# Row casts of the DMA-turned attention steps on GpSimd, and earlier query products in the indexer

## The reference

```python
q_lat = rmsnorm(hidden_states @ q_a_w, q_a_norm_w)
q = (q_lat @ q_b_w).reshape(b, s, H, QKD).transpose(0, 2, 1, 3)      # 32 heads, 128 + 64 (rope)
kv = (rmsnorm(kv_lat, kv_a_norm_w) @ kv_b_w)...
scores = (q_nope @ k_nope^T + rope(q_pe) @ rope(k_pe)^T) * QKD ** (-0.5)
idx_scores = einsum(iw, relu(iq @ ik^T)) * IDX_D ** (-0.5)           # 16 indexer heads of 128
_, topk_idx = top_k(where(causal, idx_scores, -inf), 128)
attn = softmax(where(topk_mask & causal, scores, -inf))
x = x + (attn @ v) @ o_w + experts(xn)                                # top 2 of 8, rank 16
```

## Time and profile before

| | |
|---|---|
| median of 3 runs | 975.35 us |
| the profiled execution | 986.95 us, of which the span is 985.2 us |
| PE busy | 842.8 us (86%), granted clock 0.96 over the span |
| DVE busy | 703.7 us (71%) |
| ACT busy | 654.1 us (66%) |
| POOL busy | 462.3 us (47%) |
| DMA transposes (L443) | 64 |

### The profile page before, as it was taken

The page is one execution under the profiler, slowest core; times in us unless marked ns, Lnnn a source line. Parts: engine busy times, 40 slices in busy tenths (PEclk is TensorE's granted clock), DMA queues, the critical chain, the costliest instruction groups (busy, mean ns, idle before and its releaser), DMA issues.

```text
span 985.2 us, 20194 instructions
## 1 busy us (share of the span) xinstructions
PE 842.8 (86%) x7496; PEld 502.2 (51%) x7496; DVE 703.7 (71%) x1589; ACT 654.1 (66%) x1388; POOL 462.3 (47%) x343
## 2 busy tenths in 40 slices
PE   4969989876666989888988999999999998829998
PEld 2436444443334555555554665665666665614443
DVE  5366678899999999999997777777777767620100
ACT  3657789865664878788877877887877887820000
POOL 2193388853443555455554556556556555310000
PEclk9999999978896999999999999999999999959999
DMA  7012111112332444444441665565775555670211
GB/s 231 22 44 86 55 54 44 59 38 61 99 90 65 124 125 124 117 124 118 135 123 45 135 129 118 115 120 106 130 133 118 113 118 111 119 227 1 64 43 43
DMA packets 168609, 96.66 MB, mean 98 GB/s; under 512 B 116544, under 2 KB 142528, under 8 KB 168512
## 3 DMA queue, kind: packets, MB, share of 16 engines
q1 hardware_dynamic: 168512, 95.37, 39.9%
HBM read 36.62 MB, written 6.29 MB: 44 GB/s over the span
## 4 chain that ended last, share of the span: by engine, by line
PE 44%; DVE 26%; issue 11%; ACT 10%; POOL 7%; DMA 2%; SPq 0%; POOLq 0%; DVEq 0%; ACTq 0%
PE psS L690 9%; PE psS L762 9%; DVE arena L1236 6%; DVE arena L1041 6%; ACT arena L793 6%; PE psT L746 5%; DVE m L1173 3%; POOL bias L1415 3%; DVE bias L1180 2%; PE psS L577 2%; PE psT L564 2%; PE psT L544 2%; ACT arena L978 2%; POOL arena L1349 2%; PE psO L717 2%
## 5 line engine op out<-in xcount | busy, mean ns | idle before, releaser
L690 PE MATMUL psS<-keyT,arena 128*128 128x512 f16 (+3 forms) x1152 | 231.4, 329 | 18.8 <-DVE small L1236 14.8
L978 ACT ACTIVATE arena<-arena,small 128x512 f32<-128x512 f32 (+7 forms) x256 | 198.2, 774 | 66.3 <-DVE small L1241 37.5
L1041 DVE SCALAR_TENSOR_TENSOR arena<-psT,arena 128x512 f16<-128x512 f32 (+3 forms) x278 | 146.8, 548 | 107.1 <-ACT arena L793 105.9
L793 ACT ACTIVATE arena<-psT 128x512 f16<-128x512 f32 (+4 forms) x360 | 171.8, 505 | 49.6 <-PE psT L613 25.5
L1236 DVE CUSTOM_DVE_ANT_0 arena<-psS,bias 128x512 f32<-128x512 f32 (+7 forms) x256 | 191.9, 750 | 0.1
L577 PE MATMUL psS<-ikT,big 128*128 128x512 f16 (+3 forms) x528 | 112.0, 359 | 38.1 <-DVE bias L1126 34.6
L746 PE MATMUL psT<-ident,arena 128*128 128x128 f32 x736 | 115.9, 278 | 22.1 <-DVE arena L1041 18.1
L690 PEld LDWEIGHTS psS<-keyT,arena 128*128 128x128 f16 x1152 | 91.4, 98 | 75.1 <-DVE small L1236 18.0
L1415 POOL TENSOR_TENSOR bias<-arena,bias 128x768 f32<-128x768 f32 (+2 forms) x48 | 91.3, 1916 | 58.4 <-ACT arena L859 58.1
L746 PEld LDWEIGHTS psT<-ident,arena 128*128 128x128 f32 x736 | 84.6, 141 | 55.2 <-ACT arena L978 30.9
L577 PEld LDWEIGHTS psS<-ikT,big 128*128 128x128 f16 x528 | 51.2, 104 | 91.2 <-DVE bias L1126 42.3
(11 more groups left out here) (162 smaller groups left out, 1406.5 us busy)
## 6 DMA issues: line engine op xcount, KB each, us to landing
arena<-arena SPq DMA_DIRECT2D x192, 128.0 KB, 2.4
arena<-in_wiq SPq DMA_DIRECT2D x32, 256.0 KB, 2.7
arena<-in_ow SPq DMA_DIRECT2D x16, 512.0 KB, 3.5
arena<-in_qbT SPq DMA_DIRECT2D x16, 256.0 KB, 2.5
wvo_parts<-arena SPq DMA_DIRECT2D x16, 256.0 KB, 2.0
arena<-in_qpe SPq DMA_DIRECT2D x16, 128.0 KB, 2.9
arena<-in_x SPq DMA_DIRECT2D x8, 256.0 KB, 3.3
out<-arena SPq DMA_DIRECT2D x8, 256.0 KB, 2.1
```

The source lines that it names most:

```text
L690: last = mm(bank[:, k:k + w], Q[:, u % 2, h, a, q:q + P], keyT[:, b, h, k:k + w], start=(a, b) == (0, 0), stop=(a, b) == (1, 0))
L793: return nc.scalar.activation(dst, src, ACT.Copy, scale=scale)
L978: nc.scalar.activation(pr[:, g % 4, 0:kw], pr[:, g % 4, 0:kw], ACT.Exp, bias=shift[:, g % 4:g % 4 + 1], scale=-1.0, accum_out=rsum[:, unit ...
L1041: return v.scalar_tensor_tensor(out=dst, in0=src, scalar=scale, in1=hi, op0=ALU.mult, op1=ALU.subtract)
```

## The change

There are two parts. The first takes the fp16 row cast of the 64 DMA-turned steps out of ScalarE's program and puts it into GpSimd's, straight ahead of the subtraction of the same row; the wait for the row buffer to be free goes with it. The second moves the query jobs of the first two units to other heads of the indexer's last third, and with them the swaps and placings in SyncE's order and GpSimd's and ScalarE's steps for them.

```diff
-        FIRST = {4: ("R", 0), 6: ("L", 0), 9: ("R", 1), 12: ("L", 1)}
+        FIRST = {2: ("R", 0), 4: ("L", 0), 7: ("R", 1), 10: ("L", 1)}
...
                 load_qw(p, p % 2, False)
-                if p == 7:
+                if p == 5:
                     swap(0)
+                if p == 8:
+                    place(0, latent, qa_lo, q_lat, 1)
                 if p == 10:
-                    place(0, latent, qa_lo, q_lat, 1)
+                    swap(1)
+                if p == 11:
                     place(0, turned, q_rot, q_tur, 0)
-                if p == 13:
-                    swap(1)
...
-                if n in (8, 13):
-                    rope_hi((8, 13).index(n))
+                if n in (7, 12):
+                    rope_hi((7, 12).index(n))
...
-            def rows_hi_(g):
-
-                kw, d = P * (tile_of(g) + 1), TURN_AT[g]
-                if d >= 3:
-                    act.wait_ge(landed[(d - 3) % 4], landed_by(d - 3))
-                act.wait_ge(exp_done, g + 1)
-                copy(rows_of_turn(d)[:, 0:kw], pr[:, g % 4, 0:kw], 1.0).then_inc(row_hi, 1)
...
                     exp_step(g + AHEAD - 1)
-                    if turns(g + AHEAD - 1):
-                        rows_hi_(g + AHEAD - 1)
...
             def rows_lo_(x):
                 kw, d = P * (tile_of(x) + 1), TURN_AT[x]
+                if d >= 3:
+                    pool.wait_ge(landed[(d - 3) % 4], landed_by(d - 3))
+                pool.wait_ge(exp_done, x + 1)
+                g.tensor_copy(rows_of_turn(d)[:, 0:kw], pr[:, x % 4, 0:kw]).then_inc(row_hi, 1)
                 pool.wait_ge(row_hi, d + 1)
...
-                if n in (6, 11):
-                    rope_cos((6, 11).index(n))
-                    rope_sin((6, 11).index(n))
+                if n in (4, 9):
+                    rope_cos((4, 9).index(n))
+                    rope_sin((4, 9).index(n))
+                if n in (6, 12):
+                    q_low((6, 12).index(n))
                 if n in (8, 13):
-                    q_low((8, 13).index(n))
                     rope_low((8, 13).index(n))
```

More of the change, by code:

```diff
@@ L1005, in _ @@
                 exp_step(g)
-                if turns(g):
-                    rows_hi_(g)
             for g in range(STEPS):
```

## The result

The changed kernel is 0.67% faster: the ratio of its times to those of before is 0.9933, with a 95% interval of 0.9911 to 0.9955 (20 runs of each; medians 972.86 and 979.94 us, means 973.60 and 980.22, which give that ratio). That is 6.6 us, where the sum came to 14 us. The first three runs of before (975.35) lie at the fast end of its times: the twenty go from 974.81 to 988.58 us, those of the changed kernel from 970.33 to 979.38.

A forecast was written before the change was run, and what follows sets the result against it. VectorE was taken to bound the indexer's last third, TensorE attention's second half. Terms of -8 and -6 us made -14 against the profiled 986.95 us (-1.42%); that share of the timed 975.35 gave 961, range 949 to 975.

The forecast's parts named there:

- Part 2: Indexer's last third: query jobs moved to heads 2, 4, 7, 10 free three heads, 2.0 us each, 6 us gained.
- Part 1: Attention's second half: row casts moved to GpSimd save 12.2 us, 4 given back, so 8 us gained.
- the late queries: Attention's second half: the next unit's queries land after TensorE is ready, giving back 4 us, between 0 and 12.
- the chain to the R job: Attention's second half: ScalarE's 1024-column cast delays a copy, VectorE's rest and TensorE's query job, 0.81 us a unit, 12.2 us.
- Rival (a): Attention: GpSimd's cast costs as much as its subtraction, 2.13 us, so queries land late; 980 us, slower; chance 0.12.
- The margin: Attention's second half: queries land at 653.3 by the median placing, TensorE reads them at 654.04, so 0.7 us to spare.
- the other 48 casts: Attention: casts of a unit's other three turned steps are off TensorE's critical waits; their removal gains nothing.
- Head 2 is freed: Indexer's last third: the query job delays GpSimd's join 3 past VectorE's rests of head 2, gaining 2.0 us.
- Join 4 comes 7.6 us behind the accumulation of head 2: Indexer's last third: GpSimd's join of head 4 starts after VectorE's rests of head 3, gaining another 2.0 us.
- At head 4 the job of the latents has the same effect: Indexer's last third: the latent query job at head 4 frees VectorE's rests from a join, gaining 2.0 us.
- as even: Indexer's last third, from head 5 on: no net gain or loss assumed, since TensorE's granted clock changes between levels.
- Rival (b): Indexer's last third: new joins meet VectorE's rests at other heads, costing 4 us; 971 us; chance 0.15.

The follow-up runs named there:

- the queries early: Changed kernel, second half of attention: next unit's query placings ahead of step 1's transposing DMA, rope cast and rope_low also moved ahead; ratio to before 0.98.
- Without collisions: Kernel before, with GpSimd's joins in the indexer's last third adding only 64 of 1024 columns; ratio to before 0.987.

## Why the prediction was wrong, step by step

Two terms of the sum failed. Part 2 was to give 6 us and gave nothing: its chain of joins and rests was wrong from the second link on. Part 1 was to give 8 us and gave 6: the late queries were taken too small.

- **TensorE is the bound of the second half, and the 1024-column cast is on the chain to the R job: right.** The wait is gone in every unit, and the cast alone gives the effect. Its worth was 0.97 us a unit, where the idle time gave 0.81: 14.6 us in place of 12.2.
- **The cast on GpSimd: right, and cheap.** 1.04 us, forecast 1.23 (bounds 1.0 and 2.13); the four widths give 0.84 ns a column and 0.18 us fixed, where the forecast had 1.05 and 0.15. Rival (a) needed 1.8 us and falls.
- **The queries land late: right in kind, the term was too small.** 4 us forecast, 10 us measured in 13 units. The margin was worked out as 0.7 us from one unit's issue times and the median landing. But a late landing and an early TensorE add up in each unit, and the wait ranged from nothing in some units to 1.9 us in others: the four placings of one unit landed 2.5 to 4.1 us after their issue, those of another, which made no wait, 2.4 to 3.0. Why they differ stays open. A margin near zero has to be summed unit by unit, not from a median. 14.6 less 10.0 leaves 4.6 us, and part 1 as a whole came to 6 by the times, 5 to 6 by the second halves. What is missing may be the other 48 casts, costed at nothing (some 2 us by their trace). The idle times also understate both terms: with the queries early, a unit takes 19.87 us, 1.13 less than the 21.0 before.
- **VectorE is the bound of the last third, and joins stretch it: right.** Without collisions the stage is 88.4 us.
- **"Head 2 is freed": right, in each of four traces with the new places.** What that gains depends on the run: in the second trace of before w1lo of head 2 took 0.60 us, and there was only 0.3 us to gain.
- **"Join 4 comes 7.6 us behind the accumulation of head 2, thus after the rests of head 3: 2.0 again": this step failed, and with it the term of 6 us.** The join comes 7.03 us behind it and meets w2s of head 3, which is held for 2.1 us in all four traces. The 7.6 lies between the 8.6 us of the trace of before (217.22 to 225.86) and these 7.03, during which TensorE's granted clock was 0.97 to 1.00: the time from an accumulation to the next join but one hangs on that clock: from head 1's accumulation to join 3 it was 8.69 us in the first profile of before and 7.03 in the second, with the clocks of 0.63 and 1.00 shown above.
- **"At head 4 the job of the latents has the same effect": failed too.** GpSimd's `rope_sin` holds it for 1 us. The sum counted joins only; the rotary steps and `q_low`, which the change moves as well, hold VectorE in the same way, at heads 4, 5 and 9 (rests of 1.1 to 1.3 us in place of 0.29).
- **The later heads "as even": right in the mean, by the table** (9.0 us of stretching in place of 8.9 from head 7 on), after 1.3 us lost at heads 5 and 6. A gain of 1.3 us at heads 2 to 4 was thus paid back. The measured effect is 1.001 (0.9977 to 1.0044). Rival (b), that new joins meet the rests at other heads, is what happened, but it cost the gain and not 4 us more.
- **The level.** The base was read twice from few runs. The profile of before was at the slow end of its own times (986.95 us against a median of 979.94), partly by its third of 108.1 us; the three timed runs were at the fast end. The 1.2% between them was taken for the price of profiling, but it is the spread of this kernel: the changed kernel's profiled execution, 975.21 us, is one of its twenty timed runs. That 972.86 us lies in the range of 949 to 975 is in part luck, since the range hung on a base 4.6 us under the median of twenty runs. The direction, faster at 0.82, came out.

## What to carry to other kernels

Where a stage's length hangs on whether two engines' instructions meet within tenths of a microsecond, don't cost a move by one trace, and count everything that the move shifts on the engine that collides: take a second trace of the same kernel, and take away the collision itself (give the contended operation another engine) rather than shift it. When a stall of the bound engine is removed, everything that arrives for it afterwards must be early enough by that much: list each arrival's margin in every unit, DMA landings first, and look at what stands ahead of it in its queue. Here the two moves that followed from this, the placings ahead of one DMA and two small subtractions on GpSimd, brought the kernel, with the change, to 4.7% under before, where the change alone gave 0.67%.

## What the runs showed of the hardware

- A GpSimd cast from fp32 to fp16 of 128x1024 in SBUF takes 1.04 us and one of 128x640 0.72, so 0.84 ns a column and some 0.18 us beside it; ScalarE takes 1.06 and 0.74 for the same rows. The two-input subtraction of 1024 columns takes 2.13 us. The Trainium skill (GPSIMD Engine Reference, 4.1 Engine selection) puts one-input work roughly at line rate; these rows agree, as far as a cast no slower than ScalarE's can show it.
- The Trainium skill (SBUF — State Buffer, Who interferes with whom) has VectorE's instruction with two SBUF inputs contend with a GpSimd instruction that reads SBUF, and whichever comes second wait for the whole of the first. The runs agree for the case in which GpSimd came first: 2.3 us in place of 0.29 beside a join of 1024 columns, 1.25 beside a product of 512, 0.31 in the mean beside joins of 64. In the program as a whole the joins' part of this was 1.3% of the time.
- The granted clock of TensorE in one and the same 4 us of one program was 0.63 in one run and 1.00 in another.
